# Summing the scan's states by accumulating transpositions, then copying and turning back the sum

## What is computed

```
u      = silu(conv(x @ in_w.T + in_b))                # 512 channels
delta, Bm = softplus(...), ...                        # from u
deltaA = exp(delta * A)                               # token x channel x 16 states
deltaBu = delta * u * Bm
carry  = deltaA * carry + deltaBu                     # a scan over the 32 tokens
y      = carry.sum(over the 16 states) + u * D_param
out    = y @ out_w.T + out_b
```

## Time and profile before

| | |
|---|---|
| three runs | 1186.87, 1190.63, 1191.12 us (median 1190.63) |
| the profiled execution | 1189.54 us, its span 1186.7 us |
| TensorE, VectorE, ScalarE, GpSimd busy | 88%, 80%, 61%, 61% of the span |
| granted TensorE clock, mean | 0.93 |

### The profile page before, as it was taken

One profiled execution on the slowest core, in us unless ns is written; L12 is line 12 of the kernel. 1 busy time (PEld: TensorE's weight loads), 2 busy tenths in 40 slices (PEclk: granted clock), 3 DMA queues, 4 the chain that ended last, 5 costly groups with the idle time before them and its releaser, 6 DMA issues.

```text
span 1186.7 us, 13165 instructions
## 1 busy us (share of the span) xinstructions
PE 1040.9 (88%) x4244; PEld 525.2 (44%) x4266; DVE 947.6 (80%) x1296; ACT 721.3 (61%) x1289; POOL 723.1 (61%) x506
## 2 busy tenths in 40 slices
PE   3776599899999999999999999999999999787846
PEld 3342244354545445454545454545444454433423
DVE  2632288789998999889898999899988998799743
ACT  1113455677667776767678667777677667655343
POOL 1000597777665976496659767687649664988100
PEclk8666699999999999999999999999999999989955
DMA  8400640254008220525035401731061304100100
GB/s 309 160 34 18 267 178 1 85 217 149 31 18 303 75 104 19 201 102 179 1 119 202 178 1 46 275 127 52 18 263 76 144 0 145 52 0 1 36 0 18
DMA packets 22059, 124.72 MB, mean 105 GB/s; under 512 B 3495, under 2 KB 4135, under 8 KB 9448
## 3 DMA queue, kind: packets, MB, share of 16 engines
q1 hardware_dynamic: 17384, 90.34, 20.4%
q10 hardware_dynamic: 4608, 33.56, 7.6%
HBM read 115.23 MB, written 8.65 MB: 104 GB/s over the span
## 4 chain that ended last, share of the span: by engine, by line
PE 52%; DVE 18%; ACT 11%; POOL 9%; issue 7%; DMA 2%; SPq 0%; ACTq 0%; DVEq 0%; POOLq 0%
PE bank L889 29%; PE acc L889 19%; DVE state L769 7%; POOL state L504 5%; POOL rstd L484 2%; ACT decay L555 2%; ACT soft L541 2%; PE bank L977 2%; ACT hid L541 1%; DVE sg L811 1%; ACT hid L574 1%; DVE u L881 1%; DMA brep<-b_scratch 1%; DVE raw L752 1%; DVE hm L821 1%
## 5 line engine op out<-in xcount | busy, mean ns | idle before, releaser
L504 POOL TENSOR_TENSOR state<-w,brep 128x512 f32<-128x512 f32 (+1 forms) x352 | 611.8, 1766 | 131.1 <-PE acc L889 128.2
L769 DVE TENSOR_TENSOR_SCAN state<-decay,state 128x512 f32<-128x512 f32 (+1 forms) x352 | 586.6, 1693 | 51.9 <-ACT decay L555 39.1
L889 PE MATMUL acc<-state,ident 128*128 128x512 f32 x1024 | 494.4, 607 | 20.4 <-DVE state L769 16.4
L555 ACT ACTIVATE decay<-delta,neg_a 128x496 f32<-128x496 f32 x512 | 328.5, 669 | 121.5 <-DVE state L769 121.1
L889 PEld LDWEIGHTS acc<-state,ident 128*128 128x128 f32 x1024 | 183.8, 192 | 213.0 <-issue 166.1
L528 POOL TENSOR_TENSOR w<-delta,u 128x512 f32<-128x512 f32 x32 | 40.4, 1264 | 112.7 <-ACT delta L677 112.7
L481 POOL TENSOR_TENSOR ve<-mv,eps 128x4 f32<-128x4 f32 x24 | 4.8, 199 | 148.8 <-DVE mv L756 148.8
L889 PE MATMUL bank<-xn_t,in_w 128*128 128x512 f32 x128 | 64.9, 653 | 12.2 <-DVE u L881 10.8
L584 ACT ACTIVATE sg<-bank,ag 128x512 f32<-128x512 f32 x64 | 43.7, 683 | 35.2 <-PE bank L889 35.2
L811 DVE SCALAR_TENSOR_TENSOR sg<-sg,bank 128x512 f32<-128x512 f32 x64 | 42.9, 671 | 27.2 <-ACT sg L584 27.2
L889 PE MATMUL bank<-out_w,u 128*128 128x256 f32 x256 | 57.4, 382 | 6.7 <-DVE u L760 6.7
(11 more groups left out here) (135 smaller groups left out, 1332.1 us busy)
## 6 DMA issues: line engine op xcount, KB each, us to landing
keys<-in_keys_t SPq DMA_DIRECT2D x32, 1028.0 KB, 5.6
keys<-in_keys_n SPq DMA_DIRECT2D x32, 1024.0 KB
brep<-b_scratch ACTq DMA_DIRECT2D x32, 1024.0 KB, 6.4
x_in<-in_x SPq DMA_DIRECT2D x8, 512.0 KB, 7.6
x_scratch<-x_in SPq DMA_DIRECT2D x8, 512.0 KB, 2.6
res<-x_scratch SPq DMA_DIRECT2D x8, 512.0 KB, 3.3
out<-res SPq DMA_DIRECT2D x8, 512.0 KB, 6.8
brep<-in_w_gateT SPq DMA_DIRECT2D x1, 1024.0 KB, 12.2
```

Of the source, the lines that this page charges most:

```text
L504: nc.gpsimd.tensor_tensor(state[state_buffer(odd, g)][:, 0:count, :], w[:, m, :].unsqueeze(1).to_broadcast((P, count, TOK)), brep[:, n:n + ...
L555: last = nc.scalar.activation(decay[:, to + i, :, 1:LEN], d, ACT.Exp, scale=neg_a[:, m, n + i:n + i + 1])
L769: nc.vector.tensor_tensor_scan(flat, decay[:, of:of + count, :, :].rearrange("p c q l -> p (c q l)"), flat, 0.0, ALU.mult, ALU.add).then_i ...
L889: return nc.tensor.matmul(o, l, r, start=first, stop=last)
```

## The change

TensorE adds the states up another way. Each state is cut into four groups of 128 tokens, and each group is the stationary operand of a transposition (the identity is moving, 128 columns), so a state takes four instructions of 128 columns where it took one matmul of 512. They accumulate in `acc`, which then holds the sum turned: tokens on the partitions, channels along the row. ScalarE copies it to a new buffer y_t (copy_sums), TensorE turns it back into `acc` by four transpositions (turn_sums), and VectorE's y reads it there as before.

The places change with it. Within a tile ScalarE's copy of the tile before stands after the exp of its third chunk (COPY_AT = 2), TensorE's turn at its second chunk (TURN_AT = 1), y after VectorE's third scan (Y_AT = 2), and TensorE sums the first three chunks together when it comes to the third (SUM_AT = 2), after y. For the last tile of a block there are new pieces sum_copy and sum_turn at steps 0 and 1, and y_last goes from step 0 to 2, out_proj from 1 and 2 to 3 and 3, x2 from 1 and 5 to 4 and 5.

```diff
-Y_AT = 0
+COPY_AT = 2
+TURN_AT = 1
+Y_AT = 2
+SUM_AT = 2
...
+    ("sum_copy", [0]),
+    ("sum_turn", [1]),
+    ("y_last", [2]),
...
-    ("out_proj", [1, 2]),
-    ("x2", [1, 5]),
+    ("out_proj", [3, 3]),
+    ("x2", [4, 5]),
...
+                def copy_sums(block_, m):
+                    reach(act, summed, block_, (m + 1) * CPT)
+                    reach(act, sums_turned, block_, m)
+                    nc.scalar.activation(y_t[:, :], acc[:, :], ACT.Copy).then_inc(sums_copied, 1)
...
+                        if g % CPT == COPY_AT and m:
+                            copy_sums(b, m - 1)
+                    elif part == "sum_copy":
+                        copy_sums(b, TILES - 1)
...
                 def y(block_, odd, m):
-                    reach(dve, summed, block_, (m + 1) * CPT)
+                    reach(dve, sums_turned, block_, m + 1)
...
+                def turn_sums(block_, m):
+                    reach(pe, sums_copied, block_, m + 1)
+                    for q in range(GROUPS):
+                        last = nc.tensor.transpose(acc[:, q * P:(q + 1) * P], y_t[:, q * P:(q + 1) * P], ident[:, :])
+                    last.then_inc(sums_turned, 1)
...
                     if part == "chunk":
-                        m, n, count, _ = SCAN[g]
-                        if g % CPT == 0:
+                        m, c = divmod(g, CPT)
+                        if c == TURN_AT and m:
+                            turn_sums(b, m - 1)
+                        if c == SUM_AT:
...
                             reach(pe, y_ready, b, m)
-                        reach(pe, scan_done, b, g + 1)
-                        for i in range(count):
-                            last = mm(acc[:, :], ident[:, :], state[state_buffer(odd, g)][:, i, :],
-                                      n + i == 0, n + i == STATES - 1)
-                        last.then_inc(summed, 1)
+                        for k in range(c + 1) if c == SUM_AT else (c,) if c > SUM_AT else ():
+                            s = m * CPT + k
+                            reach(pe, scan_done, b, s + 1)
+                            n, count = SCAN[s][1:3]
...
+                            for i in range(count):
+                                for q in range(GROUPS):
+                                    part_t = slice(q * P, (q + 1) * P)
+                                    last = nc.tensor.matmul(acc[:, part_t], state[state_buffer(odd, s)][:, i, part_t],
+                                                            ident[:, :], start=n + i + q == 0,
+                                                            stop=n + i == STATES - 1 and q == GROUPS - 1,
+                                                            is_transpose=True)
+                            last.then_inc(summed, 1)
```

More of the change, by code:

```diff
@@ L45 @@
     ("finish", [36, 65, 72, 78]),
-    ("out_proj", [1, 2]),
-    ("x2", [1, 5]),
+    ("out_proj", [3, 3]),
+    ("x2", [4, 5]),
     ("stats3", [5]),
     ("x_evac", [13]),
-    ("y_last", [0]),
     ("scale_x", [11]),
@@ L227, in perceiver_layer @@
         z = sb("z", [P, DIM])
+        y_t = sb("y_t", [P, TOK])
         x_dbl = sb("x_dbl", [XROWS, TOK])
@@ L340, in perceiver_layer @@
         summed = sem("summed", SLOTS)
+        sums_copied = sem("sums_copied", TILES)
+        sums_turned = sem("sums_turned", TILES)
         y_ready = sem("y_ready", TILES)
@@ L920, in b_free @@
                     after(pe, hq_t_ready, b, 2 * turned)
+                def turn_sums(block_, m):
[3 more added lines that the diff above has]
+                    last.then_inc(sums_turned, 1)
                 for part, b, g, odd in slots("tensor", j, par, pre, scan, post):
                     if part == "chunk":
-                        m, n, count, _ = SCAN[g]
-                        if g % CPT == 0:
+                        m, c = divmod(g, CPT)
+                        if c == TURN_AT and m:
+                            turn_sums(b, m - 1)
+                        if c == SUM_AT:
                             reach(pe, y_ready, b, m)
-                        reach(pe, scan_done, b, g + 1)
-                        for i in range(count):
-                            last = mm(acc[:, :], ident[:, :], state[state_buffer(odd, g)][:, i, :],
-                                      n + i == 0, n + i == STATES - 1)
-                        last.then_inc(summed, 1)
+                        for k in range(c + 1) if c == SUM_AT else (c,) if c > SUM_AT else ():
[10 more added lines that the diff above has]
+                            last.then_inc(summed, 1)
+                    elif part == "sum_turn":
+                        turn_sums(b, TILES - 1)
                     elif part == "attn_weights":
```

## The result

The changed kernel takes 1308.88 us (median of 4 runs, 1307.42 to 1310.29), the one before 1189.45 beside it on the same chip: ratio 1.1003, 95% interval 1.0989 to 1.1018. It is 10% slower, 119 us. The prediction was 1260 us with a range up to 1298: right in direction and in its main mechanism, 49 us short in size. The profiled execution has a span of 1307.4 us at a mean granted clock of 0.844; before, it was 0.93.

A forecast was written before the change was run, and what follows sets the result against it. VectorE, not TensorE, was taken as the bound. 1189.5 us plus attn_out 43.2 and 5.4, phase ends 18.9, last phase 0.7, copies 4, clock 11.5, less 10.5 given back, made 1262, stated as 1260 us; range 1222 to 1298.

The forecast's parts named there:

- the last phase: End of the run: copy and turn added, sum faster, about +0.7 us, and 1 us for the clock.
- ScalarE's copies: Four bank copies a block on ScalarE, mostly hidden, a quarter reaching VectorE through decay: 4 us in all.
- Attn_out: Tile 2: y waits for the turn behind attn_out, VectorE idle 7.7 us; 7.2 us in each of six phases, 5.4 in phase 1.
- Phase end: Block's end: late copy and turn delay out_proj and x2, 2.7 us in each of seven phases, 18.9 us.
- What is given back: VectorE's gate and convolution waits shrink as TensorE has less work and engines catch up: 1.5 us x 7 = 10.5 us less.
- The clock term: out_proj may start at half clock after TensorE idles: 1.5 us a phase, 10.5 us, and 1 for the last phase.
- The clock rival: Transpositions don't hold the clock; attn_out and out_proj run at half clock, 72 us more, near 1325 us; chance 0.10.
- Relief wins: Rival: VectorE reaches y late enough that the turn is there; 7 us won in 7 periods, 1140 us; chance 0.10.
- The bound of 12.2 us of idle time a period: VectorE idles 12.2 us of a 127 us period, the most any relief of TensorE can win there.
- Busy time of TensorE: Sign expected in the profile: sums 0.11 us apart and TensorE's busy time down by 150 us or more.
- A period of 137 us: Sign expected in the profile: a full period grows from 127 to about 137 us.
- The waits of y: Sign expected in the profile: VectorE waits for y behind attn_out, 6 to 8 us at a time, seven times.

The follow-up runs named there:

- e1: The changed kernel with TensorE's turn one chunk earlier (TURN_AT 0), ahead of attn_out in the third tile; 1256.64 us.
- e7: e1 with ScalarE's copy of a block's last sum ahead of the next block's first exp, and y_last, out_proj, x2 at their old steps; 1232.34 us.
- e8: e7 plus the filler: one bf16 matmul of zeros into acc ahead of each state but a tile's first; 1217.36 us.
- e12: e8 with copy, y and joint sums one chunk earlier in tiles 1 and 3, and sums from the first chunk in tile 0; 1206.38 us.
- e10: The kernel before with only the places within a block moved; matmul sums, no copy or turn; 1238.71 us.
- e11: The kernel before with only the phase end's places moved (y_last, out_proj, x2); matmul sums, no copy or turn; 1237.14 us.
- e4: The changed kernel's places, all of them, with matmul sums as before and no copy or turn; 1262.15 us.
- e9: The changed kernel plus the filler, a bf16 matmul of zeros ahead of each state but a tile's first; 1307.07 us.
- e3: The kernel before with transposing sums alone, not copied or turned back, all places as before; result differs; 1205.64 us.
- e5: e3 plus the filler, a bf16 matmul of zeros ahead of each state but a tile's first; 1182.37 us.
- e13: e3 with every state transposed twice into acc; 1190.46 us.
- e6: The kernel before, matmul sums kept, plus the filler ahead of each state's matmul but a tile's first; 1246.92 us.
- e14: e12 without the filler; 1237.63 us.

## Why the prediction was wrong

The 119 us by the chain of experiments, each against the one before it: turn ahead of attn_out 52 (e1), phase end 24 (e7), filler for the clock 15 (e8), places within a block 11 (e12), and 17 left. The steps overlap (e10 and e11 add up to more than e4; the filler is worth nothing in e9 and 31 in e12), so these are prices in this order. The trace of after tells the same by place, in distances of scans over the whole run: the seven phase ends 37.0 us, the seven attn_outs 51.4, the seven convolutions 20.5; the start, the last block and the last phase hold most of what is left, about 11 (1.7 had been predicted for the last phase, and 4 for ScalarE's copies).

- **Attn_out: right.** 7.7 us of stall were worked out and 7.85 stand in the trace; the period loses 7.7 there (7.2 predicted), and the seven together 52 us (48.6 predicted).
- **Phase end: mechanism right, size too small.** out_proj was put 6.3 us behind the last scan and stands at 6.9. But the half clock of it was taken as 1.5 us, and it is 9.99 - 7.17 = 2.8 (the last sums ahead of it ran slow too, 20 records in 4.20 us). x2's second half comes 6.0 us later than before, of which later work hides little: 5.5 a period, against 2.7 + 1.5.
- **"What is given back": this step failed.** It took 1.5 us off each period, since gate and convolution wait for TensorE and TensorE has less to do. The convolution got 3.7 us longer instead. Less work between its waits cost TensorE the clock just where VectorE waits for every record (e3; undone by e5 and by e13). Over the seven periods it is 20.5 us lost where 10.5 were to come back: 31 of the 49 us missing. The clock term looked at out_proj alone, because only that had a new idle time.
- **The clock rival: right that half clock matters, wrong in why and where.** It had transpositions not counting (e13 refutes it) and doubled attn_out, which took 6.9 us at full clock in after too. Its 1325 us is near the result by luck.
- **Relief wins: refuted.** With nothing added it loses 17 us (e3), and 8 are won where a filler holds the clock (e5). The bound of 12.2 us of idle time a period was right and far from reached.
- **Busy time of TensorE** fell by 78.5 and not 150 us: sums at 0.11 us apart only in full clock, and out_w and in_w records longer.
- A period of 137 us was predicted; it is 143.8, in others 143.3. The waits of y came seven times as said (6.2 and six times 7.9), and two smaller ones, 2.2 and 3.0, at the end.
- Two readings of the prediction are in the trace but not in the rows that it names: the convolution's wait of 0.9 us (the earlier trace rows has three others), and the granted clock of 1.00 behind the slow stretch of phase 8 (1035.8 to 1039.0 us; the earlier trace rows ends before). Neither changes the sum.

The last 17 us are in part placed. In e12 the seven convolutions lose 13.9 us, and the granted clock is 1.00 in five of the six full ones, 1.4 to 1.7 us each; the wait there is the one of e10, GpSimd held by the sums that stand together (VectorE waits 2.15 us for decay in these five, in e10 2.76; before 0.47), though e10 has no copy and no turn. In the table's period TensorE is at half clock besides, from 723.1 to 726.5 us, and 3.2 us are lost. Open: how much of the rest is ScalarE's copy and how much y's place. No run separates these.

## What to carry to other kernels

An engine that is busy for 88% may be no bound, and making its work shorter can cost: here TensorE, with less to do, idled longer ahead of matmuls that others wait for and came to them at half clock (in e3 3.01 us of idle where it was 0.48, and 5.37 us for the 3.67 of before). So when a change relieves TensorE, look for the stretches in which it then waits ahead of matmuls on the path, and price these at half clock. The Trainium skill (TensorE: Matmul & The Clock Gate, HAM oscillation — how this bites in real kernels) tells of a kernel whose matmuls come in short stretches with DMA waits between them, so that the clock falls in each wait, and advises to do more of the matmuls before waiting. The runs here agree, in a kernel that was made lighter: 0.873 in e3, and 0.928 and 0.939 with more work between the waits (e5, e13).

A sum that has to pass another engine and come back is priced by what stands ahead of each leg in each queue: here one place in a table was worth 52 us, and the lighter sums under 8 (e5). Follow the buffers too: sums that are put off hold GpSimd, and what stands behind it there is late (2.3 us a period in e4 and e10).

## What the runs showed of the hardware

- f32 transpositions of 128x128 follow each other after 0.11 us at full clock and 0.21 at half (in after, twenty in 4.20 us), and sums of them alone hold the clock as those of matmuls do (e13 0.939, before 0.93).
- A kernel can get faster by work that does nothing: 480 bf16 matmuls of zeros, 0.22 us each, are worth 23 us in e3's order and 31 in e14's, nothing in after's, and cost 57 us where TensorE is full (e6).
- A kernel whose clock falls in some periods and not in others varies from run to run: e14's four runs go from 1232 us at 0.885 to 1247 us at 0.871.
